# Attention on one core: twelve of the first sixteen transferred squares sent, four copied by ScalarE, and a third home for transfers

## The reference

```python
y = ((xg - mu) * jax.lax.rsqrt(var + EPS)).reshape(B, C, H, W)      # 4 groups of 32 channels
y = y * gn_gamma[None, :, None, None] + gn_beta[None, :, None, None]
qkv = jnp.einsum('bchw,dc->bdhw', y, w_qkv) + b_qkv[None, :, None, None]
q, k, v = jnp.split(qkv, 3, axis=1)
scores = jnp.einsum('bnc,bcm->bnm', q, k) * C ** (-0.5)
w = jax.nn.softmax(scores, axis=-1)
a = jnp.einsum('bnm,bmc->bnc', w, v)
out = jnp.einsum('bchw,dc->bdhw', a, w_out) + b_out[None, :, None, None]
return x + out
```

## Time and profile before

| | us |
|---|---|
| median of 3 runs | 138.07 |
| lowest, highest | 136.94, 138.17 |
| profiled execution, its time | 138.07 |
| profiled execution, its span | 136.3 |
| PE busy | 129.4 |
| DVE busy | 99.8 |
| ACT busy | 65.0 |
| POOL busy | 41.4 |

### The profile page before, as it was taken

How to read it: one execution, slowest core, us unless ns; L and a number is a source line. 1 busy time by engine, 2 the same in 40 slices (tenths; PEclk the granted TensorE clock), 3 DMA queues, 4 the chain that set the end, 5 groups by cost and what they waited for, 6 DMA issues and landing times.

```text
span 136.3 us, 1759 instructions
## 1 busy us (share of the span) xinstructions
PE 129.4 (95%) x543; PEld 89.1 (65%) x543; DVE 99.8 (73%) x170; ACT 65.0 (48%) x117; POOL 41.4 (30%) x49
## 2 busy tenths in 40 slices
PE   6999999998999949999999999999999999999990
PEld 6987688875777526666666666666656577554670
DVE  0589699999998996877686889866868886761302
ACT  3154778854675372544542475544633474730000
POOL 6032130730022229300190058000770367303210
PEclk9999999999999999999999999999999999999999
DMA  4940000030056978985689656888888459961011
GB/s 152 350 191 0 0 5 0 3 77 0 0 111 147 210 188 236 207 203 169 154 204 206 204 114 160 191 195 224 203 202 201 122 123 209 209 176 77 0 77 77
DMA packets 8937, 19.01 MB, mean 139 GB/s; under 512 B 3040, under 2 KB 3040, under 8 KB 8928
## 3 DMA queue, kind: packets, MB, share of 16 engines
q1 hardware_dynamic: 8640, 18.63, 53.8%
q10 hardware_dynamic: 288, 0.27, 0.6%
HBM read 4.20 MB, written 2.11 MB: 46 GB/s over the span
## 4 chain that ended last, share of the span: by engine, by line
PE 75%; DVE 12%; SPq 7%; issue 2%; DMA 2%; DVEq 0%
PE mixed L833 31%; PE scores L778 7%; SPq L255 7%; PE scores L779 7%; PE scores L781 7%; DVE scores L577 5%; PE scores L839 4%; PE turned L798 3%; DVE flipped_odd L605 3%; PE turned L723 3%; DMA home_odd<-flipped_odd 2%; PE mixed L830 1%; PE mixed L828 1%; PE mixed L829 1%; PE mixed L723 1%
## 5 line engine op out<-in xcount | busy, mean ns | idle before, releaser
L577 DVE TENSOR_SCALAR_CACHE_REDUCE scores<-scores,key_bias 128x1024 f32<-128x1024 f32 x31 | 40.0, 1289 | 15.0 <-PE scores L781 14.7
L426 ACT ACTIVATE probs<-scores,neg_max 128x1024 f32<-128x1024 f32 x32 | 35.7, 1116 | 22.7 <-DVE scores L577 21.9
L833 PE MATMUL mixed<-home_odd,v 128*128 128x512 f32 x48 | 22.6, 594 | 1.9 <-DMA home_odd<-flipped_odd 1.9
L833 PE MATMUL mixed<-home_even,v 128*128 128x512 f32 x48 | 22.1, 594 | 0.0
L778 PE MATMUL scores<-y_hi_odd,z_hi_odd 128*128 128x512 f32 x32 | 18.7, 585 | 0.6 <-DVE z_lo_odd L544 0.6
L778 PE MATMUL scores<-y_hi_even,z_hi_even 128*128 128x512 f32 x30 | 15.9, 531 | 0.0
L605 DVE STREAM_TRANSPOSE flipped_odd<-probs 128x1024 f32<-128x1024 f32 x12 | 14.8, 1235 | 0.3 <-DMA home_odd<-flipped_odd 0.3
L605 DVE STREAM_TRANSPOSE flipped_even<-probs 128x1024 f32<-128x1024 f32 x12 | 14.8, 1234 | 0.0
L833 PEld LDWEIGHTS mixed<-home_even,v 128*128 128x128 f32 x48 | 8.9, 189 | 7.8 <-issue 7.2
L833 PEld LDWEIGHTS mixed<-home_odd,v 128*128 128x128 f32 x48 | 8.5, 190 | 8.3 <-issue 8.0
L779 PE MATMUL scores<-y_lo_odd,z_hi_odd 128*128 128x512 f32 x32 | 12.6, 392 | 0.0
(11 more groups left out here) (162 smaller groups left out, 202.9 us busy)
## 6 DMA issues: line engine op xcount, KB each, us to landing
home_odd<-flipped_odd SPq DMA_DIRECT2D x48, 128.0 KB, 2.4
home_even<-flipped_even SPq DMA_DIRECT2D x48, 128.0 KB, 2.4
out_dram<-result SPq DMA_DIRECT2D x8, 256.0 KB, 3.5
inv_wide<-inverse_rows SPq DMA_DIRECT2D x7, 256.0 KB, 3.6
xs<-in_x_dram SPq DMA_DIRECT2D x2, 512.0 KB, 6.5
xs<-in_x_dram SPq DMA_DIRECT2D x3, 256.0 KB, 4.6
xs<-in_x_dram ACTq DMA_DIRECT2D x1, 256.0 KB, 3.3
ws<-in_weights_dram SPq DMA_DIRECT2D x1, 256.0 KB, 4.0
```

Of the source, the lines that this page charges most:

```text
L426: act.activation(probs[:, i % RING, :], scores[:, i % 2, :], ACT.Exp, bias=neg_max[:, i:i + 1], scale=-1.0, accum_out=row_sum[:, i:i + 1]) ...
L577: dve.tensor_scalar(scores[:, i % 2, :], scores[:, i % 2, :], key_bias[:, b % 2, i:i + 1], None, ALU.subtract, ALU.min, accum_out=neg_max[ ...
L833: mm = pe.matmul(bank, v[:, b % 2, k, :], there, start=first, stop=final)
```

## The change

Three things are changed. The first swapped group (1) sends 12 squares by DMA in place of 16: k runs from 1. Its four diagonal squares are copied by ACT, each 32 partitions x 1024 elements, `flipped_odd` to `home_1`, one behind the exponentials in each of the steps 8 to 11 (b == 1, i = 0 to 3); `mix` of group 1 waits for all four on a new semaphore, and so does `flip` of group 3. Third, there are three homes in place of two: group g uses home g mod 3, so that `swap` of group g waits only for the mixing of group g - 3. The room for it comes from `first_turned`, which now lies where `home_0` lies.

```diff
-        first_turned = sb("first_turned", [128, KT, HALF])
...
-        home = sb("home_even", [128, GROUP]), sb("home_odd", [128, GROUP])
+        with nc.sbuf_tensor("first_turned", [128, KT, HALF], fp32) as first_turned:
+            pass
+        home_0 = sb("home_0", [128, GROUP])
+        home = home_0, sb("home_1", [128, GROUP]), sb("home_2", [128, GROUP])
...
+        def squares_sent(group):
+
+            return SQ * (SQ - 1) if group == SWAPPED[0] else SQ * SQ
...
-            return SWAP * len([g for g in SWAPPED if g <= group and g % 2 == group % 2])
+            return sum(16 * squares_sent(g) for g in SWAPPED if g <= group and g % HOMES == group % HOMES)
...
             def swap(group):
                 sp.wait_ge(s_flipped, QB * group)
-                if group > 2:
-                    sp.wait_ge(s_mixed, KT * (group - 1))
-                for k in range(SQ):
+                if group >= HOMES:
+                    sp.wait_ge(s_mixed, KT * (group - HOMES + 1))
+                for k in range(1 if group == SWAPPED[0] else 0, SQ):
...
+            def diagonal(g):
+                act.wait_ge(s_flipped, QB)
+                act.activation(home[1][32 * g:32 * g + 32, g * N:(g + 1) * N],
+                               flipped[1][32 * g:32 * g + 32, g * N:(g + 1) * N], ACT.Copy).then_inc(s_diagonal, 1)
...
                     if after(b, i, 2)[0] < BATCHES:
                         exponentials(*after(b, i, 2))
+                    if b == 1 and i < SQ:
+                        diagonal(i)
                     if i == (1 if b == 0 else 2) and not last:
                         y_head(b + 1)
...
             def flip(n):
                 group, u = n // QB, n % QB
                 dve.wait_ge(s_exp, n + 1)
+                if group == 3:
+                    dve.wait_ge(s_diagonal, SQ)
                 if group > 2:
-                    dve.wait_ge(s_swapped[group % 2], swaps(group - 2))
+                    dve.wait_ge(s_swapped[(group - 2) % HOMES], swaps(group - 2))
...
                         if group in SWAPPED:
-                            pe.wait_ge(s_swapped[g], swaps(group))
+                            pe.wait_ge(s_swapped[group % HOMES], swaps(group))
+                            if group == SWAPPED[0]:
+                                pe.wait_ge(s_diagonal, SQ)
```

More of the change, by code:

```diff
@@ L47, in attention_kernel @@
     PAIRS = KT // 2
-    SWAP = 16 * SQ * SQ
+    HOMES = 3
     MIX = {4: [(0, 1)], 5: [(0, 1)], 6: [(0, 1)], 7: [(0, 1)], 8: [(0, 1)], 9: [(0, 1)], 10: [(0, 2)]}
@@ L189, in attention_kernel @@
         s_flipped = sem("squares_flipped")
-        s_swapped = [sem("squares_swapped_even"), sem("squares_swapped_odd")]
+        s_diagonal = sem("first_diagonal_squares_copied")
+        s_swapped = [sem(f"squares_swapped_{k}") for k in range(HOMES)]
         s_mixed = sem("mixed_tiles_done")
@@ L249, in swap @@
                 sp.wait_ge(s_flipped, QB * group)
-                if group > 2:
-                    sp.wait_ge(s_mixed, KT * (group - 1))
-                for k in range(SQ):
+                if group >= HOMES:
+                    sp.wait_ge(s_mixed, KT * (group - HOMES + 1))
+                for k in range(1 if group == SWAPPED[0] else 0, SQ):
                     for g in (0, 2, 1, 3):
                         t = g ^ k
-                        sp.dma_start(home[group % 2][32 * t:32 * t + 32, g * N:(g + 1) * N],
+                        sp.dma_start(home[group % HOMES][32 * t:32 * t + 32, g * N:(g + 1) * N],
                                      flipped[group % 2][32 * g:32 * g + 32, t * N:(t + 1) * N]
-                                     ).then_inc(s_swapped[group % 2], 16)
+                                     ).then_inc(s_swapped[group % HOMES], 16)
             def store(group):
@@ L433, in turned_copy @@
                     return
-                act.wait_ge(s_swapped[1], swaps(5))
+                act.wait_ge(s_swapped[5 % HOMES], swaps(5))
                 for j in range(2):
@@ L831, in mix @@
                     else:
-                        there = home[g][:, :].rearrange("p (g v u c) -> p v u g c", g=SQ, v=KT, u=QB)[:, k, :, :, :]
+                        there = home[group % HOMES][:, :].rearrange("p (g v u c) -> p v u g c", g=SQ, v=KT, u=QB)[:, k, :, :, :]
                         mm = pe.matmul(bank, v[:, b % 2, k, :], there, start=first, stop=final)
```

## The result

| | before | changed |
|---|---|---|
| median us | 137.72 (4 runs) | 142.85 (4 runs) |
| lowest, highest | 136.94, 138.17 | 142.46, 143.37 |
| profiled execution: time, span | 138.07, 136.3 | 142.86, 141.1 |

The ratio is 1.0376, with a 95% interval of 1.0332 to 1.0420: 5.1 us slower. The forecast was 140.4 (139.2 to 142.6). The direction and the wait for the fourth copy are as forecast; the size is more than twice the 2.3 us. The ratios compare fast executions: a few slower ones of the kernel before and of experiment 1, most of them with a fallen clock, are left out, while in all other kernels executions with a fallen clock count.

A forecast was written before the change was run, and what follows sets the result against it. PE was taken as the bound, without idle time after 51.00 us. From 138.07 us, -1.85 for the DMA wait and +4.15 for the wait on ACT's copies gave +2.30, so 140.4 us, range 139.2 to 142.6.

The forecast's parts named there:

- PE bound behind 51 us, the start of one tile decides: PE has no idle time after 51.00 us, so any shift of group 1's first tile reaches the end one for one.
- The transfers, -1.85 us: Four issues fewer on SP land the last square at 48.32 us, removing PE's 1.85 us wait for the DMA.
- The copies' order, 4.15 us of wait: On ACT the fourth copy stands behind block 13's exponentials and ends at 53.30 us; PE, ready at 49.15, waits 4.15 us.
- 0.94 for the distance between starts: On ACT, a copy of 1.04 us lets the next instruction start 0.94 us after its own start, overlapping about 0.1.
- A 32-partition copy at 1.04 us: Each diagonal copy on ACT costs 1.04 us, like a 128-partition row with the same 1024 elements per partition.
- The rival of cheap copies: ACT copies of 32 partitions cost only 0.38 us by element count: +1.1 us, 139.2 us; chance 0.08.
- The third home, nothing: Later groups' squares can start sooner, but PE waits for none of them; alone it was forecast as no change.
- The clock, chance 0.20: Rival: PE's clock falls in the longer wait and costs 2.0 us more, giving 142.4 us; chance 0.20.
- Nothing in the trace has PE idle for 4 us: Remark in the clock rival: the granted clock reads full in all 40 slices, also through PE's 1.85 us gap.
- warm-up matmuls at the lower pace: The span's first 20 PE matmuls stand 0.232 us apart against 0.130 later, losing 2.0 us though the clock reads full.
- What else moves, nothing: Delays of flip, scale, y_head and POOL's work, and earlier squares, were to open no PE wait and add nothing.
- given back later: Rival: PE absorbs part of the shift after 51.00 us, giving 138.5 to 139.4 us; chance 0.05.

The follow-up runs named there:

- experiment 1: Changed kernel with only the third home kept: all 16 squares of group 1 by DMA, no copies; 137.97 us, ratio 1.0003 to the kernel before.
- experiment 3: Changed kernel with 16 blank matmuls on PE ahead of the tile's wait for squares and copies; 140.94 us, ratio 1.0261 to the kernel before.
- 9: Changed kernel with 13 squares by DMA and three copies on ACT, two behind block 10's exponentials, one behind block 11's; 136.12 us, ratio 0.9905 to the kernel before.
- 10: Changed kernel without copies: 13 squares issued by SP, three diagonal squares issued as DMA by ACT; 137.06 us, ratio 0.9981 to the kernel before.
- Experiment 5: Changed kernel with the four ACT copies two behind block 10's exponentials and two behind block 11's; 136.93 us, ratio 0.9927 to the kernel before.
- experiment 6: Changed kernel with the four copies on POOL instead of ACT; 139.97 us, ratio 1.0141 to the kernel before.
- 2: Changed kernel with two homes instead of three, keeping 12 squares and four copies; 142.86 us, ratio 1.0405 to the kernel before.
- 4: Kernel before, with group 1's first tile also waiting for block 13's exponentials, no copies; 139.16 us, ratio 1.0146 to the kernel before.
- experiment 7: Changed kernel with the four copies in reverse order, 3, 2, 1, 0; 142.82 us in one execution.
- 8: Changed kernel with y_head of that batch moved behind the fourth copy; 141.61 us, ratio 1.0266 to the kernel before.

## Why the prediction was right or wrong

- **PE bound behind 51 us, the start of one tile decides: right.** After 53.98 PE has no wait in the changed kernel either. From the tile's start to the span's end it is 85.1 to 85.3 us in the four traced kernels that kept the clock and have no later wait (before, 3, 9, 10), 85.8 and 86.0 in the two with a later wait (5, 6), and 86.8 to 88.0 in those where the clock fell (changed, 1, 2, 4, 7, 8), so that the fall cost 1.6 to 2.8 us.
- **The transfers, -1.85 us: right.** Group 1's issues end at 46.94, 2.2 us sooner than before where 2.54 was reckoned, and PE's wait for a DMA is gone. Experiment 5 cashes it: no wait ahead of the tile and 0.39 given back, 1.5 us by the waits and 1.0 by the medians.
- **The copies' order, 4.15 us of wait: right in kind, 0.55 us short.** The tile came at 53.98 instead of 53.30. Of the 0.68, 0.13 lay ahead (PE was ready at 49.28, not 49.15). The step that failed is the one that took "0.94 for the distance between starts" and 1.10 from exponentials to the next instruction: the overlap of 0.1 us was read off rows that all begin at partition 0. Around the third copy and ahead of the fourth it is missing (49.53 behind 49.51, 50.61 behind 50.58, 52.79 behind 52.76): the three distances were 0.12, 0.14 and 0.12 us longer than taken. From the end of the copy to the tile went another 0.14, which the sum left out though the earlier trace rows has the same 0.14 behind the DMA.
- **A 32-partition copy at 1.04 us: right** (1.04 to 1.06). The rival of cheap copies falls. The estimate of 1.04 from the Trainium skill ("ScalarE: Activation LUTs", "What ACT_TABLE_LOAD costs") came true as well.
- **The third home, nothing: right** (experiment 1).
- **The clock, chance 0.20: this was the larger error.** The sum put the clock at nothing. It fell in 4 of 4 executions and cost 1.6 to 1.9 us (experiment 3); the rival had 2.0. The step that failed is the weighing. "Nothing in the trace has PE idle for 4 us" was taken as a reason for doubt, where it should have taken away the trust in the full clock of the rows. The one sign that the trace gave, warm-up matmuls at the lower pace behind an idle start, pointed the right way. With the clock in the main case the sum would have been 142.4, and with the 0.68 of the later tile 143.1; 142.85 was measured. The upper bound of 142.6 had room for the clock and none for the gaps beside it.
- **What else moves, nothing: right.** No PE wait opened behind the tile, and of what "given back later" hoped for nothing was seen.

## What to carry to other kernels

When a copy takes the place of a transfer, look up what the copy stands behind on its engine: here the same four instructions cost 5.1 us or gain 1.0, and what decides is whether the last stands behind work that itself waits for the engine one wants to free. A new wait of TensorE that is longer than any in the trace should be priced with the lower clock behind it as the likely case; some blank matmuls into a bank that is about to be restarted get that part back. And when transfers are the limit, ask whether it is the issues or what they move: here a second queue took 0.7 us off the wait, three squares fewer 1.6.

## What the runs showed of the hardware

- ACT instructions overlap by 0.1 us when both start at partition 0; next to one on partitions 32 and up they don't (experiment 7: 52.81 against 52.91, and 43.91 against 43.89).
- ACT takes 1.04 to 1.06 us for 32 or 128 partitions of 1024 elements, SBUF to SBUF; POOL takes 2.8 us for 32 and 1.2 for 128 (experiment 6). Why POOL does is open.
- A PE wait of 1.8 to 2.9 us lets the clock fall in some executions of the same kernel and not in others (traced in experiments 1 and 4, at 1.6 and 1.8 us each by the time from the tile to the end). The kernel before has a like wait, and its three executions with a fallen mean clock, 139.5 to 140.1 us, are probably the same; none of them was traced.
